# Mamba block and ternary FFN: the FFN's third layer by weight quarters over all four token tiles, two of them behind the output projection

## The reference

```python
x = layernorm(x + mamba(x))     # in_proj, causal conv, selective scan over 16 states, gate, out_proj
x = layernorm(x + ffn(x))       # ternary weights, below

def ffn(x):                     # 256 -> 1024 -> 1024 -> 1024 -> 256
    h = silu(tlin(x, w1)) * tlin(x, w2)
    h = gelu(tlin(h, h1))
    h = gelu(tlin(h, h2))
    return tlin(h, w3)          # the third layer of this document
```

## Time and profile before

| | us |
|---|---|
| median of 3 runs (2790.53 to 2793.53) | 2791.72 |
| the profiled execution's own time | 2790.6 |
| its span | 2788.8 |
| PE busy | 2443.8 (88%) |
| DVE busy | 2435.8 (87%) |
| ACT busy | 2106.6 (76%) |
| POOL busy | 1623.6 (58%) |
| mean granted TensorE clock | 0.942 |

### The profile page before, as it was taken

How to read it: one execution, slowest core, us unless ns; L and a number is a source line. 1 busy time by engine, 2 the same in 40 slices (tenths; PEclk the granted TensorE clock), 3 DMA queues, 4 the chain that set the end, 5 groups by cost and what they waited for, 6 DMA issues and landing times. The chain is left out here.

```text
span 2788.8 us, 36144 instructions
## 1 busy us (share of the span) xinstructions
PE 2443.8 (88%) x12034; PEld 1850.7 (66%) x12034; DVE 2435.8 (87%) x2402; ACT 2106.6 (76%) x3205; POOL 1623.6 (58%) x1572
## 2 busy tenths in 40 slices
PE   4466998989899898989989898998989999898988
PEld 2335675766767576676757667675766767576767
DVE  7798899899999989998998999999898999989730
ACT  5576887969788796978969697896969789696711
POOL 1224755665675666567566656756665576666544
PEclk6568999999999999999999999999999999999999
DMA  7968898988889898888989889898988889898933
GB/s 263 268 131 178 202 223 199 234 208 211 211 208 223 201 233 208 208 210 210 224 203 230 210 208 212 206 225 204 230 208 205 209 213 227 201 229 203 241 108 117
DMA packets 226798, 581.68 MB, mean 209 GB/s; under 512 B 25920, under 2 KB 26304, under 8 KB 226128
## 3 DMA queue, kind: packets, MB, share of 16 engines
q0 software_dynamic: 73728, 268.47, 52.1%
q1 hardware_dynamic: 152880, 310.84, 33.3%
HBM read 301.86 MB, written 20.45 MB: 116 GB/s over the span
## 5 line engine op out<-in xcount | busy, mean ns | idle before, releaser
L770 DVE TENSOR_TENSOR_SCAN scan_ps<-dA,scan_ps 128x1024 f32<-128x1024 f32 x416 | 951.9, 2288 | 127.4 <-PE scan_ps L408 112.4
L977 POOL DMA_DIRECT2D y<-hC x512 | 449.3, 878 | 695.7 <-DVE hC L781 547.0
L635 ACT ACTIVATE dB<-duT,bT 128x512 f32<-128x512 f32 x1024 | 715.1, 711 | 131.5 <-PE scan_ps L408 131.5
L408 PE MATMUL scan_ps<-ident,dB 128*128 128x128 f32 x4096 | 578.2, 288 | 150.3 <-DVE hC L781 124.6
L626 ACT ACTIVATE dA<-delta,a_neg 128x512 f32<-128x512 f32 (+1 forms) x1024 | 692.3, 711 | 1.1
L521 PE MATMUL ffn_ps<-hb_hi,ring 128*128 128x512 f32 x1536 | 654.5, 426 | 36.6 <-POOL hb_lo L1016 20.0
L408 PEld LDWEIGHTS scan_ps<-ident,dB 128*128 128x128 f32 x4096 | 499.8, 148 | 266.8 <-DVE hC L781 103.2
L521 PE MATMUL ffn_ps<-hb_lo,ring 128*128 128x512 f32 x1536 | 611.9, 398 | 0.0
L781 DVE TENSOR_TENSOR hC<-scan_ps,c_rows_sb 128x1024 f32<-128x1024 f32 x416 | 507.2, 1219 | 38.4 <-DMA c_rows_sb<-c_rows 8.2
L521 PE MATMUL ffn_ps<-ha_hi,ring 128*128 128x512 f32 x1024 | 437.1, 427 | 7.4 <-POOL ha_lo L1016 4.6
L521 PE MATMUL ffn_ps<-ha_lo,ring 128*128 128x512 f32 x1024 | 402.0, 393 | 0.0
(11 more groups left out here) (99 smaller groups left out, 3161.2 us busy)
## 6 DMA issues: line engine op xcount, KB each, us to landing
y<-hC POOLq DMA_DIRECT2D x512, 512.0 KB, 5.9
ring<-rounded_weights SPq DMA_DIRECT2D x704, 256.0 KB, 4.1
c_rows_sb<-c_rows SPq DMA_DIRECT2D x256, 256.0 KB, 4.6
x<-ffn_w SPq DMA_DIRECT2D x22, 512.0 KB, 6.8
rounded_weights<-ffn_w SPq DMA_DIRECT2D x22, 512.0 KB, 9.0
xt<-x_chan SPq DMA_DIRECT2D x16, 512.0 KB, 3.9
xt<-x_tok SPq DMA_DIRECT2D x16, 512.0 KB, 4.8
out_st<-x_chan SPq DMA_DIRECT2D x16, 512.0 KB, 4.2
```

The costliest lines, as they stand in the source:

```text
L408: mm = nc.tensor.transpose(dst[:, j * P:(j + 1) * P], src(j), ident[:])
L635: nc.scalar.activation(dB[:, n % 2, t, :], duT[:, t, :], ACT.Copy, scale=bT2[:, par, t, n:n + 1]).then_inc(dB_ready, 1)
L770: nc.vector.tensor_tensor_scan(states, dA[:, a:a + 2, :].rearrange("p a l -> p (a l)"), b, 0.0, ALU.mult, ALU.add).then_inc(scan_done, 1)
L977: pool.dma_start(y2[:, par, c:c + 2, :], hC[:, slot], accum_op=ALU.add).then_inc(y_added[p % 2], 16)
```

## The change

The third layer's two loops are exchanged. One call now handles one quarter of the weights for all four token tiles (`w3_quarter`), so that both PSUM tiles are filled at once and no tile is complete before the last quarter. Quarters 0 and 1 stay at steps 10 and 11, quarters 2 and 3 go to steps 17 and 18. `E_SCALE`, `E_ADD`, `E_STATS`, `E_NORM` and the store move to later steps, and each ring slot is loaded for the next row as soon as its own quarter is done.

```diff
-E_W3 = (10, 11, 13, 14)
-E_SCALE = (12, 17)
-E_ADD = (14, 19)
-E_STATS = (15, 21)
-E_NORM = 22
+E_W3 = (10, 11, 17, 18)
+E_SCALE = (19, 20)
+E_ADD = (20, 21)
+E_STATS = (21, 22)
+E_NORM = 24
...
-X_FRONT_AT, OUT_AT = 22, 24
+X_FRONT_AT = 22
+OUT_AT = 27
...
                 if used < 0:
-                    return E_W3[-1]
+                    return E_W3[QUARTERS + used]
...
                     if used < 0:
-                        wait_past(sp, pe_w3, f * TT)
+                        wait_past(sp, pe_w3, f * QUARTERS + (used + 1))
...
-            def w3_tile(f, t, full):
-
-                job = 4 * HC + t // 2
-                if t % 2 == 0:
-                    pe.wait_ge(gelu_x32, f * (2 * HC) + (job - 3 - 2 * HC + 1))
-                for q in range(QUARTERS):
-                    e = FIRST_W3 + (t * QUARTERS + q if full else q)
-                    if t == 0:
-                        pe.wait_ge(ffn_lo, f * FFN_TILES + (2 * HC + 2 * q + 2))
-                    if full or t == 0:
-                        wait_entry(f, e, full)
+            def w3_quarter(f, q, full):
+
+                e = FIRST_W3 + q
+                if q == 0:
+                    pe.wait_ge(gelu_x32, f * (2 * HC) + (2 * HC - 1))
+                pe.wait_ge(ffn_lo, f * FFN_TILES + (2 * HC + 2 * q + 2))
+                wait_entry(f, e, full)
+                for t in range(TT):
                     steps = [(a[:, 2 * q + k, t * P:(t + 1) * P], entry(e, full)[:, k * DIM:(k + 1) * DIM])
                              for k in range(2) for a in (ha_hi, ha_lo)]
-                    mm = products(ffn_ps[job % 3][:, (t % 2) * DIM:(t % 2 + 1) * DIM], steps, q == 0,
-                                  q == QUARTERS - 1, full)
-                    if full and q < QUARTERS - 1:
-                        mm.then_inc(pe_quarter, 1)
+                    mm = products(ffn_ps[(4 * HC + t // 2) % 3][:, (t % 2) * DIM:(t % 2 + 1) * DIM], steps,
+                                  q == 0 and t % 2 == 0, q == QUARTERS - 1 and t % 2 == 1, full)
                 mm.then_inc(pe_w3, 1)
...
                     k = E_SCALE.index(s)
-                    dve.wait_ge(pe_w3, f * TT + 2 * (k + 1))
+                    dve.wait_ge(pe_w3, f * QUARTERS + QUARTERS)
```

More of the change, by code:

```diff
@@ L198, in build @@
         pe_res, pe_out, pe_x1T = sem("pe_res"), sem("pe_out"), sem("pe_x1T")
-        pe_l1, pe_half, pe_w3, pe_quarter = sem("pe_l1"), sem("pe_half"), sem("pe_w3"), sem("pe_quarter")
+        pe_l1, pe_half, pe_w3 = sem("pe_l1"), sem("pe_half"), sem("pe_w3")
         conv_base, conv_taps = sem("conv_base"), sem("conv_taps")
@@ L265, in build @@
         FIRST_W3 = FIRST_HALF + HALVES
-        def entry_count(full):
-            return FIRST_W3 + (TT * QUARTERS if full else QUARTERS)
+        ENTRIES = FIRST_W3 + QUARTERS
         @block.sync
@@ L322, in entry_step @@
                     return HALF_AT[used - FIRST_HALF]
-                return TILES + E_W3[(used - FIRST_W3) // QUARTERS]
+                return TILES + E_W3[used - FIRST_W3]
             def load_weights(f, entries, full):
@@ L336, in load_weights @@
                     else:
[L337 to L342, removed]
+                        sp.wait_ge(pe_w3, f * QUARTERS + (used - FIRST_W3 + 1))
                     dst = full_ring[:, e % slots, :] if full else ring[:, e % slots, :].bitcast(F32)
-                    src = (ffn_w if full else w_dram)[half // 2]
-                    sp.dma_start(dst, src[:, (half % 2) * ENTRY_COLS:(half % 2 + 1) * ENTRY_COLS]
+                    src = (ffn_w if full else w_dram)[e // 2]
+                    sp.dma_start(dst, src[:, (e % 2) * ENTRY_COLS:(e % 2 + 1) * ENTRY_COLS]
                                  ).then_inc(ring_loaded[e % slots], 16)
@@ L359, in iteration @@
                     if end is not None:
-                        load_weights(end, [e for e in range(entry_count(full)) if entry_step(e, full) == s + TILES], full)
+                        load_weights(end, [e for e in range(ENTRIES) if entry_step(e, full) == s + TILES], full)
                     if tail is not None:
-                        load_weights(tail, [e for e in range(entry_count(full)) if entry_step(e, full) == s], full)
+                        load_weights(tail, [e for e in range(ENTRIES) if entry_step(e, full) == s], full)
                     if s == X_FRONT_AT and front is not None and tail is not None:
@@ L508, in wait_entry @@
                 slots = FULL_RING if full else RING
-                per_row = entry_count(full) // slots
+                per_row = ENTRIES // slots
                 pe.wait_ge(ring_loaded[e % slots], f * (16 * per_row) + 16 * (e // slots + 1))
@@ L589, in iteration @@
                     if end is not None and s in E_W3:
-                        w3_tile(end, E_W3.index(s), full)
+                        w3_quarter(end, E_W3.index(s), full)
                     if tail is not None:
```

## The result

| | before | after |
|---|---|---|
| median of 4 runs, us | 2791.12 (2788.54 to 2793.53) | 2857.35 (2854.57 to 2862.27) |
| ratio to before | | 1.0241, 95% interval 1.0229 to 1.0253 |
| profiled span, us | 2788.8 | 2858.0 |
| DVE busy, us | 2435.8 | 2484.5 |
| PE busy, us | 2443.8 | 2448.3 |

A forecast was written before the change was run, and what follows sets the result against it. The prediction took DVE's order to bound steady iterations, PE having idle time. Steady iterations -3.6, iteration 16 -1.8 and iteration 17 +0.1 gave -5.3 us; from 2791.7 that made 2786.4, rounded up to 2786.6 us, range 2781.5 to 2791.5.

The forecast's parts named there:

- steady DVE sum: Steady iterations on DVE: 0.46 us lost, 0.72 gained, NORM's 1.27 us moved at par; -3.6 us over 14 iterations.
- Scan 9's wait: Steady iterations: scan 9 no longer waits for PE's transposes, 0.63 us idle and 0.09 overlap, 0.72 us gained.
- Two adjacent products: Pairs 6 and 7: with SCALE0 and ADD0 moved away, products stand 2.42 us behind their scans; 0.46 us lost.
- first rival: Steady iterations: products close up to their scans and the whole 0.72 us wait is won; 2779.9 us, chance 0.11.
- Third rival: Quarter 3 comes late at PE's lower clock, so SCALE0 waits and holds NORM; 2805 us, chance 0.11.
- slot of pair 5: Scan 8 needs this slot; ring loads served ahead of its DMA would make it 3.6 us late; taken as nothing.
- Net -0.26 an iteration: Steady iterations on DVE: 0.46 us lost less 0.72 gained, -3.6 us over 14 iterations.
- gates met at the low clock: First FFN tile's gate or tanh: taken as 0, with mostly this behind the range's 0 to +0.3 us an iteration.
- second rival: Only the tail gains; new waits of 0.2 to 0.3 us an iteration eat the 0.26; 2790.5 us, chance 0.24.
- Tail: Iterations 16 and 17: -1.8 us with PE as the path, then about +0.1 us in the last chain; 1.7 gained.

The follow-up runs named there:

- norm22: Changed kernel with NORM back at step 22 and the statistics at steps 20 and 21; 2789.6 us, 0.9994 of before.
- before_norm24: Kernel before with only NORM moved from step 22 to 24 and the store to step 27; 2859.55 us, 1.0241 of before.
- norm24_psum: Changed kernel, NORM at step 24 reading a PSUM tile instead of `out_st`, second layer norm's output left out; 2803.71 us, 1.0044 of before.
- norm28: Changed kernel with NORM moved from step 24 to 28 and the store from 27 to 31; 2822.56 us, 1.0104 of before.
- pair14: Changed kernel with pair 12's product on VectorE and pair 14's on GpSimd, NORM still at step 24; 2846.5 us, 1.0207 of before.
- w3_early: norm22 with quarters 2 and 3 back at steps 13 and 14 instead of 17 and 18; 2824.13 us, 1.0128 of before.
- stats21: norm22 with both statistics at step 21 instead of steps 20 and 21; 2786.9 us, 0.9995 of before.
- stats21_add14: stats21 with ADD0 at step 14 instead of 15, between scan 7 and its product; 2789.38 us, 0.9999 of before.

## Why the prediction was wrong

- **The step that failed** is the last one of the steady DVE sum: NORM "lands at step 24: 1.27 us out at step 22 (1411.54 to 1412.81), the same in at 24". It is 4.38 us from start to start. norm22 and before_norm24 pin it to this step alone, norm24_psum to the SBUF source, norm28 and pair14 to the POOL instructions that lie beside it. The duration was carried over from a stretch where POOL is idle for 4.21 us. The prediction reads no row of POOL's arithmetic at the new place, and no rival has it, although the trace of before had instructions whose longest is three times their median.
- Its price: an iteration takes 4.76 us more where 0.26 less had been forecast, so 5.0 us, 14 times, is 70 us. Of the 5.0, 3.1 are NORM itself and 1.9, by difference, waits behind it. Behind the last scan the traced execution takes 3.7 us more, where 1.7 less had been forecast: NORM takes 2.68 us in iteration 16 as well, and in norm22 that stretch is 3.85 us shorter. Together this is more than the 70.7 us by which the median lies above the forecast; the traced execution was itself 2.5 us above that median.
- **Scan 9's wait, -0.72.** Right, and w3_early shows that it is the quarters' doing.
- **Two adjacent products, +0.46.** Right: 2.42 us from scan to product at both places. Pairs 6 to 8 are 0.35, 1.00 and 1.32 us shorter, 2.67 in sum, where 2.7 had been worked out. The first rival (all of the wait won) falls.
- **Third rival, quarter 3 late.** No wait of SCALE0; falls. It had the right sign, with the wrong mechanism, and its 2805 us would have been 52 too low. The range's fear for the slot of pair 5 behind the ring loads falls too: scan 8 does not wait.
- **Net -0.26 an iteration.** A second step that failed, though a small one. In the rows that had been worked out the gain is there once NORM and the statistics stand well (iteration 8 takes 162.55 us in stats21, 162.79 before), but the mean period is 163.17 against 163.01. In norm22 the gain is eaten by 0.25, since each statistic stands directly behind the addition that it reads; in stats21 by waits of 1.4 us in a few iterations and shorter ones at pair 11. The prediction took 0 for gates met at the low clock, which is what those few iterations show. That was the second rival, in part: its gates, but not in every iteration.
- **Tail.** Read in norm22 from the last scan: the add after OUT3 comes 2.06 us earlier (35.04 against 37.1; 2.5 forecast), PE's last product ends 2.0 earlier where 3.2 had been forecast (1.8 and 1.4; the 1.8 is 2.5 less 0.7 for NORM at step 24, which norm22 does not have), and behind it SCALE0, ADD0 and STATS0 take 1.86 more (1.6 forecast). The end comes 0.15 us earlier, not 1.7.

## What to carry to other kernels

A duration belongs to a place: before an instruction of VectorE is moved, read what GpSimd computes at the new place, and compare that instruction's maximum with its median in the trace, since 3 us can hide in an operation of 0.4. A measured saving on one engine is worth only what the next engine's slack allows: removing 0.7 us of hold gained nothing where ScalarE ran almost without a pause. And an exchange of two stages should be tried one half at a time; here each half moved the time by about 35 us, and they cancelled.

## What was not expected of the hardware

- A group of four instructions of 1.36 us became 2.4 to 4.5 us beside GpSimd's arithmetic (casts of 0.66 and 0.91, a subtraction of 1.26, a product of 2.38 us). In all of the NORMs read one by one (after, norm28, pair14, before_norm24) a held instruction ended 0.15 to 0.17 us after GpSimd's, whether GpSimd ran a cast, a subtraction or a product. With a PSUM source the group took 1.88 us in every iteration, and in the kernel before none of 416 products and 128 gates that read PSUM was longer than 1.227 and 0.691 us.
- Iterations that are 1.4 us longer go with a granted clock of TensorE that is high early and low just behind. Windows of stats21, two stretches of iteration 2 (1.4 us longer) and one of iteration 3, the first tile of the FFN in both cases at 430 and 594.4:

```profile
430.00:432.00 2.00, 1.80 (x8) 1.13 (x6) 2.00 (x5) 1.47 (x3) 0.00 (x0) 1.00 0.04 7
...
436.00:438.00 2.00, 2.00 (x8) 1.71 (x7) 2.00 (x2) 0.00 (x0) 1.92 (x3) 0.50 0.89 226
```

```profile
594.40:596.40 2.00, 2.00 (x6) 1.61 (x5) 2.00 (x6) 1.30 (x2) 0.00 (x0) 0.50 0.00 0
```

```profile
439.12 0.69 DVE L875 SCALAR_TENSOR_TENSOR gate<-gate,ffn_ps 128x512 f32<-128x512 f32 x1 [0.84 <-ACT gate L696]
```

In iteration 2 PE runs its first tiles at the higher level (2.4 GHz, 1.00), has to wait 1.04 and 0.73 us for DVE in between, and drops to the lower level for the second tile, for which DVE then waits 0.84 us (last row) and 0.38. In iteration 3 PE runs the first tile at the lower level without idle time, and is at the higher one when DVE needs it. The same pair of windows, one from 0.8 us ahead of the second layer norm's NORM and one from 5.2 us behind its start, 2 us each, was read in all 14 iterations of before, norm22, stats21 and stats21_add14. The six long iterations, and no others, have 1.00 and then 0.50. A high clock in the first window alone is harmless: four iterations of before have 1.00 in both and are no longer than the rest. Which of the two an iteration gets is not settled here.
